# Rows along w without padding; the transform along h as 48-column products in two column halves

## The chip, the cores and the metric

One core of a Trainium2 chip runs the whole kernel. The metric is device time in microseconds (us); less is better. Data is float32 throughout, and a float32 product appears in the trace as two MATMUL records with a LDWEIGHTS record each, so a count of x14 stands for seven products. In this text such a record is called a pass.

## The reference

The input `x` is (2, 64, 64, 384): two images of 64 x 64 positions with 384 channels. Four spectral layers follow each other. Layers 0, 2 and 3 are alike; layer 1 uses a Hartley transform over all axes.

```python
xf = jnp.fft.rfft2(x, axes=(1, 2)).reshape(B, H, W // 2 + 1, 8, 48)      # 8 blocks of 48 channels
o1r = relu(einsum(xr, w1[0]) - einsum(xi, w1[1]) + b1[0])                # per block, 48 x 48
o1i = relu(einsum(xi, w1[0]) + einsum(xr, w1[1]) + b1[1])
o2r = einsum(o1r, w2[0]) - einsum(o1i, w2[1]) + b2[0]
o2i = einsum(o1i, w2[0]) + einsum(o1r, w2[1]) + b2[1]
out = irfft2(softshrink(o2r) + 1j * softshrink(o2i)) + x                 # layer 1: _dht instead
```

## The kernel before, in words

The kernel stays in the spectrum between layers. Phase A (about 0 to 360 us) transforms the input and does layer 0; phase B (to about 600 us) is layer 1; phase C is layers 2 and 3 and the inverse transform. The change touches only phase A.

The input is worked through in `PASSES = 4` passes: two images, and of each two halves of the channels (`PASS_C = 192` channels, that is two pairs of blocks). In a pass:

- **S1** (`s1`, L866, eight units `v` per pass) is the transform along w, as 64 x 64 products. Its result is copied from PSUM to a `stage` tile by `s1_views`: one half by ScalarE (L1159), one by VectorE (L1278). SyncE stores the stage to the DRAM tensor `rows_along_w` (`store_stage`, L586); of pass 0 GpSimd's queue stores half (L805).
- In `stage` and `rows_along_w` a channel pair takes `ROWS = 112` columns: 48 channels, 16 columns of padding, 48 channels. Two pairs make `PASS_ROWS = 224`. GpSimd zeroes the padding of the first four stage tiles once (L794, semaphore `pads_zeroed`), and the first S1 copies wait for that (L1127).
- `load_bm` (L594) reads six or seven columns of the w axis back into a `Bm` tile (three slots), now with h along the partitions.
- **S2** (`s2`, L889, 40 steps) is the transform along h. In it the data are the weights: for each of the `nk` columns (7 or 6) one product with `Bm(e)[:, at, cols]`, 128 x 112, as weights and a 128 x 128 constant `dft_h` as the moving operand. The result, 112 partitions x `nk` * 128, is copied by ScalarE to `modes_a(s)` (L1159).
- **S3** (`mix_first`, L901) and **S4** (`mix_second`, L910) are the two block products of layer 0. S3 reads partitions 0 to 47 and 64 to 111. **TA** (`turn`, L920) transposes the updated modes, **5A** (`s5`, L940) is the inverse along h, **6A** (`s6a`, L951) the inverse along w for layer 1.

The order is written out by hand in `order()`. A round r of phase A issues on TensorE: S2(r), TA(r-4), in some rounds S1 or 6A, S3(r-1), 5A, S4(r-2), in some rounds again S1 or 6A; then the next round. There are four PSUM units of two banks; each unit of work takes the next, once the work four places earlier has been copied out (`take`). Every engine runs its own part of this order, and semaphores tie them. PE passes of a unit follow each other with no wait in between.

On SyncE's queue, after the stores of pass 0: the constants, `load_bm(0)`, weights of layer 0, `load_bm(1)`, `load_bm(2)`, more constants, the four parts of the input of pass 1, weights for layer 1, `fwd_c`; then in round 2 `load_bm(3)`, which waits for S2(1) alone.

Of the kernel before, what the change touches and what calls it, by code (L numbers as in the profile page):

```python
# [4 lines left out]
BS = C // NB  # L5
P = 128
NT = C // P
HP = H // 2
# [7 lines left out]
HALF = 64  # L16
ROWS = HALF + BS
PAIRS = NB // 2
LAMBDA = 0.01

GROUPS = [7, 7, 7, 6, 6]
PASS_GROUPS = len(GROUPS)
PASSES = 2 * B
PASS_C = C // 2
PASS_PAIRS = PAIRS // 2
PASS_STEPS = PASS_GROUPS * PASS_PAIRS
PASS_ROWS = PASS_PAIRS * ROWS
STEPS = 2 * PASS_STEPS
ALL_STEPS = B * STEPS
ALL_GROUPS = PASSES * PASS_GROUPS  # L30
STEP_COLS = 2 * H * max(GROUPS)
ITEMS = 2 * PASS_GROUPS

X_PARTS = 4
X_HP = HP // X_PARTS
# [6 lines left out]
Y_SLOTS = 3  # L42
STAGE_SLOTS, BM_SLOTS, D_SLOTS, TURN_SLOTS, AN_SLOTS = 3, 3, 2, 2, 2
A_SLOTS = 7
C_SLOTS, R_SLOTS = 9, 4
# [207 lines left out]
    return parts, fwd_c.reshape(FOLD_ROWS + 1, -1).astype(np.float32), inv_c.reshape(P, -1).astype(np.float32)  # L253


STAGE_COLS = X_HP * PASS_ROWS
W3, W4 = 2 * PAIRS * ROWS, NB * 2 * HALF
FWD, INV, V3, V4 = 2 * 2 * 2 * P, 2 * 2 * (FOLD + 1), 2 * PAIRS * ROWS, NB * HALF

# [1 line left out]
def build(nc, x, consts, fwd_c_dram, inv_c_dram, conv_w3, conv_w4, conv_bias, l1_w3, l1_bias, l1_q, l1_e, l1_t,  # L261
# [11 lines left out]
    with ctx:  # L273
        def sb(name, n):
            return ctx.enter_context(nc.sbuf_tensor(name, [P, n], F32))

        def sem(name):
            return ctx.enter_context(nc.semaphore(name))

        def dram(name, shape):  # L280
            return nc.dram_tensor(name, shape, F32, kind="Internal").ap()
# [1 line left out]
        spectrum = dram("spectrum", (B, C + 1, KW, 2, H))  # L283
        flipped = dram("flipped", (B, C, MODES))
        update = dram("update", (B, 2, FOLD + 1, MODES))
        rows_along_w = dram("rows_along_w", (PASSES, P, HP, PASS_ROWS))
        rows_along_h = dram("rows_along_h", (2 * PASSES, 4, HP, HP, PASS_C))
        first_mix = dram("first_mix", (P, V3))
        second_mix = dram("second_mix", (ROWS, V4))

        X_AT, STAGE_AT = 0, X_PARTS * X_HP * PASS_C
        BM_AT, BM_COLS = STAGE_AT + STAGE_SLOTS * STAGE_COLS, max(GROUPS) * PASS_ROWS
        TURN_COLS = max(GROUPS) * PASS_C
        G_COLS = HP * PASS_C
        RX = sb("RX", BM_AT + BM_SLOTS * BM_COLS)
        RA = sb("RA", (A_SLOTS + 4) * STEP_COLS)
        RD = sb("RD", (D_SLOTS + TURN_SLOTS) * TURN_COLS)
        RG = sb("RG", 2 * G_COLS)
# [7 lines left out]
        def cst(name):  # L306
# [3 lines left out]
        identity, dft_w, dft_h, inv_w, inv_w_flip = (  # L310
            cst(n) for n in ("identity", "dft_w", "dft_h", "inv_w", "inv_w_flip"))
# [8 lines left out]
        def stage(p, k):  # L320
            if (p, k) == (0, X_PARTS - 1):
                return RD[:, D_SLOTS * TURN_COLS:D_SLOTS * TURN_COLS + STAGE_COLS]
            at = STAGE_AT + (p * X_PARTS + k) % STAGE_SLOTS * STAGE_COLS
            return RX[:, at:at + STAGE_COLS]

        def Bm(e):
            at = BM_AT + e % BM_SLOTS * BM_COLS
            lo, hi = columns_of(e)
            return RX[:, at:at + (hi - lo) * PASS_ROWS].rearrange("p (k r) -> p k r", r=PASS_ROWS)

        def D(e):
            at = e % D_SLOTS * TURN_COLS
# [32 lines left out]
            return RX[:, at:at + 2 * H * step_of(s)[3]]  # L365

        b_at = (C_SLOTS + R_SLOTS) * STEP_COLS
        assert BM_AT <= b_at

        OUT_COLS = X_HP * PASS_C  # L370

# [12 lines left out]
        N = STEP_COLS // 2  # L384
# [22 lines left out]
        an1_high, = in_region(RA, 3 * PAIRS * N, [PASS_PAIRS * N])  # L407
        assert Y_SLOTS * 4 * STEP_COLS + PASS_PAIRS * N <= b_at and 3 * PAIRS * N + PASS_PAIRS * N <= A_SLOTS * STEP_COLS
        an0, kf0, c0, c1 = in_region(RX, b_at, [PAIRS * N, PAIRS * N, N, N])
        assert Y_SLOTS * 4 * STEP_COLS <= BM_AT and b_at + 2 * PAIRS * N + 2 * N <= BM_AT + BM_SLOTS * BM_COLS  # L410
        kf1, r0, r1 = in_region(RD, 0, [PAIRS * N] * 3)
        assert 3 * PAIRS * N <= (D_SLOTS + TURN_SLOTS) * TURN_COLS
        raw0, s0, s1 = in_region(RA, 0, [PAIRS * N] * 3)
# [22 lines left out]
        prep, prep_at, at = {}, {}, 0  # L436
# [10 lines left out]
        psum = ctx.enter_context(nc.psum_tensor("psum", [P, UNITS * UNIT], F32))  # L447
# [5 lines left out]
        def banks(key):  # L453
            return unit(key).rearrange("p (a n) -> p a n", a=2)
# [5 lines left out]
        consts_loaded = sem("consts_loaded")  # L460
        inverse_loaded = sem("inverse_loaded")
        lambda_set = sem("lambda_set")
        pads_zeroed = sem("pads_zeroed")
        x_loaded = [sem(f"x_loaded{k}") for k in range(X_PARTS)]
        stage_stored = [sem(f"stage_stored{s}") for s in range(STAGE_SLOTS)]
        first_stage_stored = [sem(f"first_stage_stored{k}") for k in range(X_PARTS)]
# [97 lines left out]
        def stage_views(p, k, x):  # L564
            at = (4 * k + x) * X_HP
            return (rows_along_w[p, at:at + X_HP].rearrange("y q r -> q y r"),
                    stage(p, k)[x * HP:(x + 1) * HP].rearrange("q (y r) -> q y r", r=PASS_ROWS))

        block = ctx.enter_context(nc.Block())

# [214 lines left out]
        def _(pool):  # L785
# [3 lines left out]
                pool.dma_start(flipped[p // 2, c0:c0 + PASS_C // 2], AN(p, g)  # L789
                               ).then_inc(flipped_stored[(p * PASS_PAIRS + g) % AN_SLOTS], 16)  # L790

            for k in range(X_PARTS):
                pad = stage(0, k).rearrange("p (m r) -> p m r", r=ROWS)[:, :, BS:HALF]
                nc.gpsimd.memset(pad, 0.0).then_inc(pads_zeroed, 1)  # L794
            zeros = RN[0:KW, 0:2 * H]
            nc.gpsimd.memset(zeros, 0.0).then_inc(zero_set, 1)
            pool.wait_ge(zero_set, 1)
# [2 lines left out]
            for k in range(X_PARTS):  # L800
                wait_emptied(pool, ("S1", 0, 2 * k))
                wait_emptied(pool, ("S1", 0, 2 * k + 1))
                for x in range(2, 4):
                    dst, src = stage_views(0, k, x)
# [23 lines left out]
            for z in range(ITEMS):  # L828
                q, b = z // 2, z % 2
                n0, n = sum(GROUPS[:q]) * H, GROUPS[q] * H  # L830
                for t in range(2):
                    wait_emptied(pool, ("CI", z, t))
                for sign in range(2):
                    dst = update[b, sign, 0:FOLD, n0:n0 + n].rearrange("(t p) n -> p t n", t=2)
# [14 lines left out]
        def _(pe):  # L849
# [28 lines left out]
            def s2(s):  # L878
                key, e = ("S2", s), s // PASS_PAIRS
                _, g, k0, nk = step_of(s)  # L880
                bank = take(key)
                if s == 0:
                    pe.wait_ge(consts_loaded, 16)
                if s % PASS_PAIRS == 0:
                    wait_bm_loaded(pe, e)
                cols = slice(g % PASS_PAIRS * ROWS, (g % PASS_PAIRS + 1) * ROWS)
                for k in range(nk):
                    at, of = (max(k - 1, 0), k + 1 if k < 2 else 0) if k0 == 0 else (k, 0)
                    mm = nc.tensor.matmul(bank[0:ROWS, k * P:(k + 1) * P], Bm(e)[:, at, cols], dft_h[:, of * P:(of + 1) * P],  # L889
                                          start=True, stop=True)  # L890
                mm.then_inc(filled, 1)

            def mix_first(key, layer, n, src):
# [126 lines left out]
                mm.then_inc(filled, 1)  # L1020

            pe.wait_ge(dft_w_loaded, 16)
            for key in plan.order:
                stage = key[0]
                if stage == "S1":
# [58 lines left out]

        def s1_views(key, j):
            _, p, v = key
            n = 2 * PASS_ROWS
            at = j * (STAGE_COLS // 2) + v % 2 * n
            dst = stage(p, v // 2)[:, at:at + n].rearrange("p (m r) -> p m r", r=ROWS)
            dst = bass.AP(dst.tensor, dst.offset, [list(dst.ap[0]), [ROWS, n // ROWS], [HALF, 2], [1, BS]])  # L1090
            return dst, banks(key)[:, j, 0:2 * PASS_C].rearrange("p (m b c) -> p m b c", b=2, c=BS)

        def turn_views(key, first):
            _, s = key
# [29 lines left out]

        def wait_stage_free(eng, key):
            _, p, v = key
            if p == 0 and v == 0:  # L1127
                eng.wait_ge(pads_zeroed, X_PARTS)
            m = p * X_PARTS + v // 2 - STAGE_SLOTS
            if v % 2 == 0 and p > 0:  # L1130
                wait_stage_stored(eng, m // X_PARTS, m % X_PARTS)
# [144 lines left out]
        def _(vec):  # L1276
# [146 lines left out]
            def join_s(q):  # L1423
                vec.wait_ge(s_folded, 2 * B * (q + 1))
                n = GROUPS[q] * H
                for d, op in enumerate((ALU.add, ALU.subtract)):
                    for f in range(2):
                        nc.vector.tensor_tensor(s_sum[d][:, f, :, 0:n], s_of[0][:, f, :, 0:n], s_of[1][:, f, :, 0:n], op
                                                ).then_inc(s_joined, 1)

            nc.vector.memset(small[:, 0:1], -LAMBDA).then_inc(lambda_set, 1)
            nc.vector.memset(small[:, 1:2], -LAMBDA / 64).then_inc(lambda_set, 1)
            for key in plan.order:
                stage = key[0]
# [27 lines left out]
                elif stage == "TA":  # L1462
                    _, s = key
                    e = s // PASS_PAIRS
# [14 lines left out]
                elif stage in ("5A", "5C"):  # L1479
                    at = 0 if stage == "5A" else ALL_GROUPS  # L1480
# [13 lines left out]
                elif stage == "CF":  # L1494
                    _, z, h = key
                    n = GROUPS[z // 2] * H
# [10 lines left out]
                elif stage == "H2":  # L1507
                    _, z, h = key
                    q, b = z // 2, z % 2
                    n = GROUPS[q] * H  # L1510
                    r = shrunk(h, GROUPS[q]).rearrange("p (a n) -> p a n", a=2)
# [165 lines left out]
```

## Time and profile before

| | before |
|---|---|
| median of 3 runs | 1030.41 us (1029.93 to 1033.44) |
| the profiled execution | 1035.22 us, of it the span of the trace 1033.4 us |
| TensorE busy (matmul) | 925.4 us, 90% |
| TensorE busy (weight load, beside matmul) | 466.4 us, 45% |
| VectorE, ScalarE, GpSimd busy | 574.3, 476.5, 80.7 us |
| chain that ended last, by engine | PE 79%, DMA 10%, DVE 4%, issue 3% |
| L889 (S2) matmul | x528, 71.0 us busy, 21.1 us idle just before |
| DMA moved | 184.39 MB in 94255 packets |

The profiled execution took 4.8 us more than the median. Engines are PE (TensorE matmul), PEld (its weight load), DVE (VectorE), ACT (ScalarE), POOL (GpSimd), SP (SyncE). The profile gives for groups of instructions their busy time, the mean duration of one, and the idle time of their engine just before them with what ended it.

### The profile page before, as it was taken

Reading aid. Unit: us, or ns where it says so; the run is one execution under the profiler, and the core shown is the slowest. Engines: PE = TensorE matmul, PEld = TensorE weight load, DVE = VectorE, ACT = ScalarE, POOL = GpSimd, SP = SyncE. Lnnn points to the kernel's source line nnn. Section 1 sums busy time; section 2 is a strip of 40 time slices with the busy share of each in tenths; the row PEclk is TensorE's granted clock in tenths of the full one; section 3 lists DMA queues with packets and bytes.
Section 4 is the critical chain, followed back from the end, with each engine's and each line's share of the span. In section 5 each row is a group of like instructions: output and inputs, shape, how many; then the busy total and the mean of one; then the engine's idle time right before and its main releaser. Section 6 shows DMA issues by size and latency. Waiting matters only on the chain.

```text
span 1033.4 us, 14264 instructions
## 1 busy us (share of the span) xinstructions
PE 925.4 (90%) x5168; PEld 466.4 (45%) x5168; DVE 574.3 (56%) x869; ACT 476.5 (46%) x757; POOL 80.7 (8%) x157
## 2 busy tenths in 40 slices
PE   3879999999999989499999999999999999999812
PEld 1536556665766646144444434443433434344301
DVE  1245554454544847476775676665667656656411
ACT  1435445545544424133343445655565655556501
POOL 3011111111111100000000110000000000000001
PEclk8889999999999999799999999999999999999966
DMA  8976699478658696934333443442754566451464
GB/s 277 328 204 187 249 286 356 136 201 293 224 159 281 197 313 166 210 90 123 96 105 89 128 128 106 103 131 77 237 138 138 159 211 177 137 204 49 130 127 184
DMA packets 94255, 184.39 MB, mean 178 GB/s; under 512 B 12455, under 2 KB 72129, under 8 KB 92394
## 3 DMA queue, kind: packets, MB, share of 16 engines
q1 hardware_dynamic: 84362, 142.33, 47.1%
q0 software_dynamic: 9824, 41.14, 12.1%
q8 instruction: 43, 0.70, 0.3%
q14 instruction: 26, 0.21, 0.1%
HBM read 104.29 MB, written 79.14 MB: 177 GB/s over the span
## 4 chain that ended last, share of the span: by engine, by line
PE 79%; DMA 10%; DVE 4%; issue 3%; ACT 2%; SPq 1%; DVEq 0%; POOL 0%; ACTq 0%; POOLq 0%
PE psum L910 16%; PE psum L901 16%; PE psum L940 9%; PE psum L889 6%; PE psum L977 6%; PE psum L993 6%; PE psum L1017 6%; PE psum L920 5%; PE psum L951 4%; DMA RX<-rows_along_w 4%; PE psum L1004 3%; DMA RG<-rows_along_h 3%; PE psum L866 2%; DMA RX<-spectrum 1%; ACT RA L1174 1%
## 5 line engine op out<-in xcount | busy, mean ns | idle before, releaser
L1318 DVE SCALAR_TENSOR_TENSOR RA<-psum,RA 112x896 f32<-112x896 f32 (+1 forms) x120 | 124.3, 1036 | 221.6 <-ACT RA L1174 221.4
L1174 ACT ACTIVATE RA<-psum,small 112x896 f32<-112x896 f32 (+1 forms) x120 | 115.9, 966 | 96.8 <-PE psum L910 94.3
L910 PE MATMUL psum<-RA,RW 112*64 112x448 f32 (+1 forms) x640 | 132.4, 535 | 1.4 <-ACT RA L1165 1.4
L1165 ACT ACTIVATE RA<-psum,RW 112x448 f32<-112x448 f32 (+1 forms) x160 | 89.4, 610 | 79.3 <-PE psum L901 79.3
L940 PE MATMUL psum<-RD,const 128*128 128x384 f32 (+1 forms) x304 | 100.0, 450 | 9.9 <-DVE RA L1278 5.3
L1278 DVE COPY RD<-psum 128x672 f32<-128x672 f32 (+2 forms) x122 | 69.7, 572 | 67.0 <-PE psum L940 60.7
L1159 ACT ACTIVATE RA<-psum 128x384 f32<-128x384 f32 (+2 forms) x72 | 50.6, 704 | 86.5 <-PE psum L889 59.1
L889 PE MATMUL psum<-const,RX 128*112 128x128 f32 x528 | 71.0, 289 | 21.1 <-DMA RX<-rows_along_w 21.1
L1159 ACT ACTIVATE RD<-psum 128x384 f32<-128x384 f32 (+2 forms) x122 | 64.1, 526 | 39.6 <-PE psum L940 37.8
L1303 DVE TENSOR_TENSOR RX<-RX,RA 112x768 f32<-112x768 f32 (+2 forms) x80 | 80.7, 1009 | 1.5
L889 PEld LDWEIGHTS psum<-const,RX 128*112 128x112 f32 x528 | 63.6, 186 | 39.7 <-issue 33.2
L940 PEld LDWEIGHTS psum<-RD,const 128*128 128x128 f32 x304 | 51.2, 192 | 63.7 <-issue 29.2
L910 PEld LDWEIGHTS psum<-RA,RW 112*64 112x64 f32 x640 | 39.1, 136 | 77.0 <-issue 68.6
L901 PE MATMUL psum<-RX,RN 48*112 48x448 f32 (+1 forms) x320 | 66.9, 535 | 5.8 <-issue 4.3
L901 PE MATMUL psum<-RA,RW 48*112 48x448 f32 (+1 forms) x320 | 67.0, 537 | 2.7 <-ACT RX L1159 1.7
L1165 ACT ACTIVATE RA<-psum,RN 112x448 f32<-112x448 f32 (+1 forms) x80 | 44.7, 610 | 49.1 <-PE psum L901 49.1
L901 PE MATMUL psum<-RX,RW 48*112 48x448 f32 (+1 forms) x320 | 67.0, 537 | 0.0
L910 PE MATMUL psum<-RA,RN 112*64 112x448 f32 (+1 forms) x320 | 65.2, 528 | 0.9 <-ACT RA L1165 0.9
L816 POOL DMA_DIRECT2D spectrum<-RA x80 | 40.1, 505 | 302.2 <-DVE RA L1303 213.4
L1224 ACT ACTIVATE RA<-psum,small 112x448 f32<-112x448 f32 (+1 forms) x80 | 44.7, 610 | 38.4 <-PE psum L993 38.4
L1159 ACT ACTIVATE RN<-psum 96x264 f32<-96x264 f32 (+4 forms) x52 | 30.6, 588 | 67.7 <-PE psum L1017 42.0
L977 PE MATMUL psum<-RG,RF 96*128 96x448 f32 (+3 forms) x160 | 61.8, 530 | 0.0
(102 smaller groups left out, 1092.7 us busy)
## 6 DMA issues: line engine op xcount, KB each, us to landing
RG<-rows_along_h SPq DMA_DIRECT2D x7, 3072.0 KB, 11.7
rows_along_h<-RD SPq DMA_DIRECT2D x96, 144.0 KB, 2.9
RX<-x SPq DMA_DIRECT2D x16, 768.0 KB, 8.0
out<-RA POOLq DMA_DIRECT2D x16, 768.0 KB, 4.5
rows_along_w<-RX SPq DMA_DIRECT2D x54, 224.0 KB, 5.3
rows_along_h<-RD SPq DMA_DIRECT2D x64, 168.0 KB, 3.1
RX<-rows_along_w SPq DMA_DIRECT2D x12, 672.0 KB, 6.8
spectrum<-RA POOLq DMA_DIRECT2D x48, 168.0 KB, 5.1
```

Source lines behind the costliest of these rows:

```text
L889: mm = nc.tensor.matmul(bank[0:ROWS, k * P:(k + 1) * P], Bm(e)[:, at, cols], dft_h[:, of * P:(of + 1) * P], start=True, stop=True)
L901: mm = nc.tensor.matmul(dst, w3[layer][rows, a, g], src[rows, :, a], start=a == 0, stop=a == 1)
L910: mm = nc.tensor.matmul(bank[b * HALF:(b + 1) * HALF, a * BANK:a * BANK + nk * H], w4[layer][0:ROWS, g, b, a], hidden(slot)[0:ROWS, b * N: ...
L940: mm = nc.tensor.matmul(dst, matrix[:, 0:P], d[:, at:at + hi - lo], start=True, stop=True)
L977: mm = nc.tensor.matmul(bank[:, part * BANK:part * BANK + n], fwd_c_view[rows, t, part, m], uv[d][rows, part, t, 0:n], start=t == 0, stop= ...
L993: mm = nc.tensor.matmul(bank[0:ROWS, r * BANK:r * BANK + n], v3_view[rows, s, g], src[rows, 0:n], start=s == 0, stop=s == 1)
L1159: return nc.scalar.activation(dst, src, ACT.Copy)
L1165: done = nc.scalar.activation(hidden(slot)[0:ROWS, b * N:b * N + nk * H], banks(key)[0:ROWS, b, 0:nk * H], ACT.Relu, bias=bias[layer][0:RO ...
L1174: nc.scalar.activation(dst, src, ACT.Relu, bias=minus_lambda_l0 if key[0] == "S4" else minus_lambda).then_inc(act_emptied, 1)
L1278: return nc.vector.tensor_copy(dst, src)
L1303: last = nc.vector.tensor_tensor(m[:, :, k], m[:, :, k], src[:, :, k], ALU.add)
L1318: nc.vector.scalar_tensor_tensor(out=dst, in0=src, scalar=LAMBDA / 64 if key[0] == "S4" else LAMBDA, in1=dst, op0=ALU.add, op1=ALU.min).th ...
```

## The change

A channel pair is carried in 96 columns, without the 16 of padding. Stage, `rows_along_w` and `Bm` shrink from 224 to 192 columns per row. In S2 each product of 112 weight columns becomes two of 48, one per channel block: block 0 writes PSUM partitions 0 to 47, block 1 partitions 64 to 111, of the same bank and columns, with the same moving operand. The partitions between (48 to 63) are no longer written by S2, so VectorE clears partitions 32 to 63 of all of PSUM once at the start (semaphore `psum_cleared`, for which TensorE waits before its first product); GpSimd's four memsets and `pads_zeroed` go. S1's copies write a contiguous destination. The tile `RX` keeps its size by another expression.

```diff
-PASS_ROWS = PASS_PAIRS * ROWS
-STAGE_COLS = X_HP * PASS_ROWS
+STAGE_COLS = X_HP * PASS_C
-        rows_along_w = dram("rows_along_w", (PASSES, P, HP, PASS_ROWS))
+        rows_along_w = dram("rows_along_w", (PASSES, P, HP, PASS_C))
-        BM_AT, BM_COLS = STAGE_AT + STAGE_SLOTS * STAGE_COLS, max(GROUPS) * PASS_ROWS
+        BM_AT, BM_COLS = STAGE_AT + STAGE_SLOTS * STAGE_COLS, max(GROUPS) * PASS_C
...
-            for k in range(X_PARTS):
-                pad = stage(0, k).rearrange("p (m r) -> p m r", r=ROWS)[:, :, BS:HALF]
-                nc.gpsimd.memset(pad, 0.0).then_inc(pads_zeroed, 1)
...
-                cols = slice(g % PASS_PAIRS * ROWS, (g % PASS_PAIRS + 1) * ROWS)
                 for k in range(nk):
                     at, of = (max(k - 1, 0), k + 1 if k < 2 else 0) if k0 == 0 else (k, 0)
-                    mm = nc.tensor.matmul(bank[0:ROWS, k * P:(k + 1) * P], Bm(e)[:, at, cols], dft_h[:, of * P:(of + 1) * P],
-                                          start=True, stop=True)
+                    for b in range(2):
+                        c0 = (g % PASS_PAIRS * 2 + b) * BS
+                        mm = nc.tensor.matmul(bank[b * HALF:b * HALF + BS, k * P:(k + 1) * P], Bm(e)[:, at, c0:c0 + BS],
+                                              dft_h[:, of * P:(of + 1) * P], start=True, stop=True)
...
+            pe.wait_ge(psum_cleared, 1)
...
-            n = 2 * PASS_ROWS
+            n = 2 * PASS_C
             at = j * (STAGE_COLS // 2) + v % 2 * n
-            dst = stage(p, v // 2)[:, at:at + n].rearrange("p (m r) -> p m r", r=ROWS)
-            dst = bass.AP(dst.tensor, dst.offset, [list(dst.ap[0]), [ROWS, n // ROWS], [HALF, 2], [1, BS]])
-            return dst, banks(key)[:, j, 0:2 * PASS_C].rearrange("p (m b c) -> p m b c", b=2, c=BS)
+            return stage(p, v // 2)[:, at:at + n], banks(key)[:, j, 0:n]
...
-            if p == 0 and v == 0:
-                eng.wait_ge(pads_zeroed, X_PARTS)
...
+            nc.vector.memset(psum[32:HALF, :], 0.0).then_inc(psum_cleared, 1)
             nc.vector.memset(small[:, 0:1], -LAMBDA).then_inc(lambda_set, 1)
```

## Rows read from the trace of the kernel before

**Rows 1.** Busy time by stretch: PE, PEld, DVE, ACT, POOL; granted clock, DMA share, GB/s.
```profile
10.00:25.30 15.30, 3.77 (x40) 1.51 (x32) 3.20 (x6) 2.80 (x6) 6.02 (x10) 0.76 0.96 272
...
100.00:360.00 260.00, 257.80 (x1783) 161.33 (x1780) 137.47 (x217) 127.48 (x197) 35.25 (x70) 1.00 0.74 239
```

**Rows 2.** PE's waits from 70.5 to 360 us: total, times, longest.
```profile
PE psum L889 <- DMA RX<-rows_along_w: 5.1, 1, 5.1
PE psum L951 <- DVE RN L1278: 0.9, 2, 0.7
```

**Rows 3.** The chain that ended last, pieces of its first 75 us: start, us, what.
```profile
5.67 8.14 PE psum L866 x64
...
18.59 6.54 DMA rows_along_w<-RD
25.27 4.37 DMA RX<-rows_along_w
29.78 5.87 PE psum L889 x28
35.68 34.68 DMA RX<-rows_along_w
70.50 2.87 PE psum L889 x12
```

**Rows 4.** DMA issues: queue, count, KB each, median us from issue to landing.
```profile
rows_along_w<-RX SPq DMA_DIRECT2D x54, 224.0 KB, 5.3
...
RX<-rows_along_w SPq DMA_DIRECT2D x12, 672.0 KB, 6.8
...
RX<-rows_along_w SPq DMA_DIRECT2D x8, 784.0 KB, 9.3
```

**Rows 5.** PE groups by shape (weights, then moving operand): count, busy us, mean ns, idle before.
```profile
L910 PE MATMUL psum<-RA,RW 112*64 112x448 f32 x384 | 84.1, 559 | 1.4 <-ACT RA L1165 1.4
...
L966 PE MATMUL psum<-RG,const 64*64 64x384 f32 x256 | 28.2, 538 | 22.3 <-DMA RG<-rows_along_h 22.3
```

**Rows 6.** PE and PEld around one S4 unit and the S2 after it: start, us, passes.
```profile
40.67 0.20 PEld L910 LDWEIGHTS psum<-RA,RW 112*64 112x64 f32 x4 [0.67 <-ACT RA L1159]
40.67 0.60 PE L910 MATMUL psum<-RA,RW 112*64 112x448 f32 x2
40.67 1.72 PE L910 MATMUL psum<-RA,RW 112*64 112x448 f32 x8
41.10 0.14 PEld L910 LDWEIGHTS psum<-RA,RW 112*64 112x64 f32 x2 [0.23 <-issue]
42.33 1.78 PE L889 MATMUL psum<-const,RX 128*112 128x128 f32 x14
```

**Rows 7.** PE, two stretches: of phase A, 286 to 295 us, and of phase C, 717 to 722 us.
```profile
286.34 1.56 PE L940 MATMUL psum<-RD,const 128*128 128x384 f32 x4
...
289.49 1.57 PE L951 MATMUL psum<-const,RG 128*96 128x66 f32 x16
290.90 1.73 PE L889 MATMUL psum<-const,RX 128*112 128x128 f32 x14
292.46 0.74 PE L920 MATMUL psum<-const,RA 112*128 112x112 f32 x6
...
717.70 1.72 PE L910 MATMUL psum<-RA,RW 112*64 112x448 f32 x8
719.25 1.67 PE L910 MATMUL psum<-RA,RN 112*64 112x448 f32 x8
720.86 0.89 PE L920 MATMUL psum<-const,RX 112*128 112x112 f32 x7
```

**Rows 8.** VectorE's first instruction, and two of its PSUM copies by shape (count, busy, mean ns).
```profile
0.81 0.06 DVE L1431 MEMSET small<- 128x1 f32 x1 [0.81 <-PEq L1667]
...
L1278 DVE COPY RD<-psum 128x672 f32<-128x672 f32 x2 | 1.7, 844 | 0.0
L1278 DVE COPY RD<-psum 128x384 f32<-128x384 f32 x2 | 1.1, 558 | 0.2
```

More of the change, by code:

```diff
@@ L291, in build @@
         X_AT, STAGE_AT = 0, X_PARTS * X_HP * PASS_C
-        BM_AT, BM_COLS = STAGE_AT + STAGE_SLOTS * STAGE_COLS, max(GROUPS) * PASS_ROWS
+        BM_AT, BM_COLS = STAGE_AT + STAGE_SLOTS * STAGE_COLS, max(GROUPS) * PASS_C
         TURN_COLS = max(GROUPS) * PASS_C
         G_COLS = HP * PASS_C
-        RX = sb("RX", BM_AT + BM_SLOTS * BM_COLS)
+        RX = sb("RX", max(BM_AT + BM_SLOTS * BM_COLS, (C_SLOTS + R_SLOTS + 5) * STEP_COLS))
         RA = sb("RA", (A_SLOTS + 4) * STEP_COLS)
@@ L328, in Bm @@
             lo, hi = columns_of(e)
-            return RX[:, at:at + (hi - lo) * PASS_ROWS].rearrange("p (k r) -> p k r", r=PASS_ROWS)
+            return RX[:, at:at + (hi - lo) * PASS_C].rearrange("p (k r) -> p k r", r=PASS_C)
         def D(e):
@@ L367, in build @@
         b_at = (C_SLOTS + R_SLOTS) * STEP_COLS
-        assert BM_AT <= b_at
         OUT_COLS = X_HP * PASS_C
@@ L409, in build @@
         an0, kf0, c0, c1 = in_region(RX, b_at, [PAIRS * N, PAIRS * N, N, N])
-        assert Y_SLOTS * 4 * STEP_COLS <= BM_AT and b_at + 2 * PAIRS * N + 2 * N <= BM_AT + BM_SLOTS * BM_COLS
+        assert Y_SLOTS * 4 * STEP_COLS <= BM_AT and b_at + 2 * PAIRS * N + 2 * N <= (C_SLOTS + R_SLOTS + 5) * STEP_COLS
         kf1, r0, r1 = in_region(RD, 0, [PAIRS * N] * 3)
@@ L462, in build @@
         lambda_set = sem("lambda_set")
-        pads_zeroed = sem("pads_zeroed")
+        psum_cleared = sem("psum_cleared")
         x_loaded = [sem(f"x_loaded{k}") for k in range(X_PARTS)]
@@ L566, in stage_views @@
             return (rows_along_w[p, at:at + X_HP].rearrange("y q r -> q y r"),
-                    stage(p, k)[x * HP:(x + 1) * HP].rearrange("q (y r) -> q y r", r=PASS_ROWS))
+                    stage(p, k)[x * HP:(x + 1) * HP].rearrange("q (y r) -> q y r", r=PASS_C))
         block = ctx.enter_context(nc.Block())
```

## Prediction

> **What bounds the kernel now.** I read three views first. The busy times by stretch say where TensorE has slack: from 100 to 360 us it is busy 257.8 of 260 us at full clock, while the DMA engines are at 0.74 [rows 1]. Then PE's own waits in phase A: behind 70 us they come to under 7 us, of which one of 5.1 us is for a `Bm` load, and the next in size is 0.9 us in two places [rows 2]. Then the chain that ended last, followed through the first 75 us [rows 3]: after S1 it is DMA up to 29.78 us (stores of the stage, landed at 25.1, then the first `Bm` load), TensorE to 35.68, and once more a `Bm` load, issued at 35.68 and used at 70.50. So phase A has two limits. Until 70.5 us the transfers decide: from 10 to 25.3 us the DMA engines are busy 0.96 of the time at 272 GB/s [rows 1]. After that the sum of TensorE's units decides, and every 0.1 us added to or taken from a unit goes straight to the end, 40 rounds long.
>
> The change acts on both: fewer bytes early, and other work for TensorE in each of the 40 S2 units.
>
> **Part 1, the products of S2.** What is S2 bound by? A unit of 14 passes takes 1.78 us, of which about 0.27 is the tail of the last pass, so a pass comes every (1.78 - 0.27) / 14 = 0.108 us [rows 6]. The 5A unit of full width: 4 passes of 384 moving columns in 1.56 us, (1.56 - 0.28) / 4 = 0.32 us per pass, or 0.83 ns per column [rows 7]; 128 columns times that is 0.107. So S2 is bound by the 128 moving columns, not by its 112 weight columns. Two products of 48 weight columns stream the same 128 columns twice. If they ran one after the other, S2's time would double; if the two column halves of the array work side by side, it stays.
>
> The nearest row is S4 (L910): 64 weight columns, outputs at partitions 0 and 64 of the same bank, the two halves next to each other in program order. Eight passes of 448 columns take 1.72 us; at 0.83 ns per column one pass needs 0.373 us, so eight in a row would take 3 us. The window of 0.1 us from the start of the unit already holds two passes, and a weight load of two more runs at 41.10 beside the matmuls [rows 6]. Over the whole run it is 84.1 / 384 = 0.219 us per pass; with four quarters (the inverse along w of phase C, L966, 64 x 64) it is 28.2 / 256 = 0.110 us per pass of 384 columns, against the 0.32 of full width [rows 5, 7]. The array runs tiles at different output partitions at once. S2's new products differ from S4's in three points: 128 instead of 112 contraction rows, 48 instead of 64 columns, and a stream of 128 instead of 448, so that 4 passes and 4 loads must be fed per 0.215 us. Feeding is no problem by the same rows: 4 loads and the 2 first passes begin within 0.1 us. I take the pair's pitch at 0.108 us as before, and +0.3 us in 40 units for the second half starting a few ns later. Bounds of this part: 0 and, if serial, 264 products x 2 passes x 0.108 = +57 us.
>
> **Part 2, the neighbours of S2.** Going from one shape of tile to another costs TensorE a pause. S4 before S2: its streams end at 40.67 + 0.05 (first load) + 4 x 0.375 (a pair of passes: 448 columns at 0.83 ns and 2 ns) = 42.22, S2 begins at 42.33, 0.10 later, and then takes 1.78 us, where the S2 behind a 6A of full width takes 1.73 [rows 6, 7]. S2 before TA, both of full width: TA begins at 292.46, 1.56 after S2's start, just when 14 x 0.109 and a part of the first load are over: no pause [rows 7]. Two units in column halves: 717.70 + 0.05 + 1.50 = 719.25, the next begins at 719.25, and takes 1.67 instead of 1.72. A turn behind column halves: 719.25 + 1.50 = 720.75, it begins at 720.86, 0.10 later, and takes 0.89 us for 7 passes, where 0.74 for 6 and one more of 0.10 make 0.84 [rows 7]. After the change S2 belongs to the column halves. By the order:
> - S2 to TA, 36 times, 34 of them behind 70 us: + (0.10 + 0.05) x 34 = +5.1 us.
> - S4 to S2, 17 times, 16 behind 70 us: the pause of 0.10 goes, and so does the exposed first load of 112 columns, 0.09 (1.78 less 0.27 less 13 x 0.109): -0.19 x 16 = -3.0 us.
> - 6A to S2, 9 times: a pause of 0.10 instead of some 0.03, and 0.04 of first load as before: +0.07 x 9 = +0.6 us.
> - S1 (or the one weight product) to S2, 8 times behind 70 us: the pause stays, the exposed load shrinks from 0.09 to 0.04: -0.4 us.
>
> With the 0.3 of part 1 that is +2.6 us. These sit on the path, since PE doesn't wait there [rows 2]; what falls before 70 us is swallowed by the wait for the load. Bounds: 0, if all is absorbed, and +6 us, if nothing is saved at S4 to S2.
>
> That such a pause exists is also what the Trainium skill states, in TensorEngine Tiling (Array Packing), section Key Properties: a change of tiling mode drains the engine, a change of tile within one mode does not. It gives no figure, and the rows here agree with both halves of it; the sum goes by the rows.
>
> **Part 3, the bytes.** Each row goes from 224 to 192 columns, one seventh less. Sixteen stores of pass 0 at 224 KB [rows 4] are 3.67 MB, 0.52 MB less after; at 272 GB/s [rows 1] that is 1.9 us of the stretch that ends at 25.1 us. Of the first `Bm` load, 672 KB in 4.37 us from issue to use [rows 3, 4], 0.1 MB goes: 0.2 us. If time went by number of pieces and not by bytes it would be 0, as the count stays. Bounds 0 to 2.3; I take 2.1, since that stretch is at the DMA engines' limit. The second place is the load issued at 35.68. It stands behind everything queued since 25 us, so it shifts with the start (the 2.1 again, not added), and 0.33 MB less lies in front of it and in it: at 272 GB/s up to 1.2 us, at the least 0; I take 0.7. TensorE itself arrives there 2.1 us earlier, so the wait stays, some 4.5 us long instead of 5.1, and what is won by both is 2.8 us. Behind it nothing in phase A waits on a transfer, so the lighter DMA traffic there is worth 0.
>
> **Part 4, the start.** VectorE clears 4096 columns on 32 partitions before anything else. Its copies of 672 and 384 columns out of PSUM take 844 and 558 ns [rows 8]: 0.99 ns per column, so 4096 take about 4.2 us, from 0.81 to 5.0. TensorE's first pass waits for the input until 5.67 [rows 3]; this covers it with 0.5 us to spare. ScalarE's `lambda_set` comes 4.2 us later and is not needed before the first S1 result at 7.4. If the clearing took twice as long, the start would move by 3.7 us, though part of it would go into stores that wait for the DMA engines anyway. The memsets that GpSimd loses had ended before 2 us and nobody waited on them. S1's copies keep their 384 elements: 0. The copy of S2 keeps its shape: 0.
>
> **Sum,** on the profiled execution of 1035.22 us: -2.8 + 2.6 = -0.2 us. Moved to the median of the runs shown, 4.8 us lower: 1030.4 - 0.2 = 1030.2 us. About 0.5% (5 us) is what a measurement can tell from no change here.
>
> **Rivals.**
> 1. Serial halves (slower). If two products of 128 rows over the same moving columns don't share the array, S2 doubles: +57 us, 1087. For it: no row shows 128 contraction rows in column halves, or one operand streamed into both. Against it: S4 does it with 112 rows. It decides from the first S2 on.
> 2. Weight loads no longer hidden. With a stream of only 0.107 us and a load of 48 columns on each side, a load that can't overlap adds its 0.04 us (6A: 16 passes of 96 weight columns in 1.57 us, 0.083 each and longer than the 0.055 of its 66 moving columns, so 0.86 ns per weight column [rows 7]): 528 x 0.04 = +21 us, 1051. Against it: the load at 41.10 runs beside matmuls in S4. This is what a rule of the Trainium skill would give (TensorE: Matmul & The Clock Gate, the mechanism of packing small matmuls: weight loads overlap matmuls in flight only where the row groups differ). In S4 all row groups are shared and the load overlaps, so the trace speaks against it.
> 3. The early transfers give more. If the load at 35.68 lands early enough that the 5.1 us wait goes, and S2 behind it runs at 2.4 instead of 1.2 GHz (2.87 us for 12 passes against 1.73 for 14), it is 5.1 + 1.3 + 2.1 - 2.6 = -6 us, 1024. Against it: 0.33 MB can't pay for 5 us.
> 4. The change saves bytes but not time (time by pieces): 0 + 2.6, 1033. This lies within the forecast's case.
>
> **How the numbers follow.** Forecast with rival 4, that is all within 0.5%: 0.74. Rival 3: 0.10. Rival 1: 0.08; rival 2: 0.04; the clearing at the start or more pauses than counted, beyond +5 us: 0.04. So faster by over 0.5% 0.10, same 0.74, slower 0.16. The parts' own bounds reach from -3.5 to +6 us; rival 3 extends the lower end. The range is 1023.5 to 1036.5 us.
>
> **What would show it.** L889 at x1056 with a busy time near 71 us and two passes beginning together; an S2 of seven columns in about 1.7 us. Near 130 us busy would be rival 1, near 92 rival 2. TA behind S2 at 0.79 us and 0.1 us later; S4 to S2 with no pause. First S2 at about 27.7 us, the seventh at about 67.7. A first S1 pass later than 5.7 us would mean that the clearing isn't covered.

## The result and the profile after

The change makes the kernel slower by 0.2 to 0.3%: 1034.62 us (median of 20 runs) against 1031.86 (20 runs), a ratio of 1.0031 [1.0017, 1.0044]. The same kernel timed twice more, each time beside the kernel before, gave 1.0012 [0.9998, 1.0026] and 1.0018 [1.0007, 1.0030]; weighted by their intervals the three make 1.0020 ± 0.0007, or +2.1 ± 0.8 us. Executions in a slow state with a lower granted clock (one of `e10_flips_together` with 1561.73 us, one of the kernel before with 1052.01) are left out of all ratios. The forecast was -0.2 us. The time is inside the range of 1023.5 to 1036.5 us and inside the half per cent called "same", but the effect is clear of zero, and it has the other sign.

The profiled execution of after took 1034.76 us (span 1033.0), that of before 1035.22. The two profiles therefore don't show the difference; the profiled before lay 3.4 us above the median of its kernel, the profiled after on it. What they do show is each step by itself. First the page of after: busy times, DMA totals, and S2 (L885 now, L889 before) with its weight loads.

```profile
PE 924.8 (90%) x5696; PEld 464.0 (45%) x5696; DVE 577.8 (56%) x870; ACT 476.4 (46%) x757; POOL 79.5 (8%) x153
...
DMA packets 94131, 180.26 MB, mean 175 GB/s; under 512 B 12455, under 2 KB 72001, under 8 KB 92266
...
L885 PE MATMUL psum<-const,RX 128*48 128x128 f32 x1056 | 68.9, 284 | 20.6 <-DMA RX<-rows_along_w 20.6
L885 PEld LDWEIGHTS psum<-const,RX 128*48 128x48 f32 x1056 | 61.0, 128 | 36.0 <-issue 29.1
```

Twice as many passes, 1056, hold TensorE for 68.9 us. That is 0.065 us a pass, where 128 columns take 0.107 us to stream: the two halves work side by side. Next, TensorE around an S2 behind an S4, and around one behind a 6A and ahead of TA (start, us, line, weights, moving operand, passes).

```profile
38.52 1.72 PE L906 MATMUL psum<-RA,RW 112*64 112x448 f32 x8
40.08 1.70 PE L885 MATMUL psum<-const,RX 128*48 128x128 f32 x28
...
288.91 1.57 PE L947 MATMUL psum<-const,RG 128*96 128x66 f32 x16
290.42 1.74 PE L885 MATMUL psum<-const,RX 128*48 128x128 f32 x28
292.08 0.79 PE L916 MATMUL psum<-const,RA 112*128 112x112 f32 x6
```

S4 to S2 is 1.56 us from start to start, 1.66 before, and S2 takes 1.70 instead of 1.78 [rows 6]. 6A to S2 is 1.51, 1.41 before; S2 to TA is 1.66, 1.56 before; TA takes 0.79 instead of 0.74 [rows 7]. Then VectorE's first instructions, the chain that ended last up to the seventh S2, and PE's waits from 68.7 to 360 us.

```profile
1.66 3.47 DVE L1424 MEMSET psum<- 32x4096 f32 x1 [1.66 <-PEq L1661]
5.13 0.06 DVE L1425 MEMSET small<- 128x1 f32 x1
```

```profile
5.58 7.21 PE psum L861 x64
...
16.73 6.91 DMA rows_along_w<-RD
...
23.77 3.90 DMA RX<-rows_along_w
...
27.80 5.74 PE psum L885 x56
...
33.58 34.92 DMA RX<-rows_along_w
...
68.63 2.80 PE psum L885 x24
```

```profile
PE psum L885 <- DMA RX<-rows_along_w: 5.6, 1, 5.6
PE psum L897 <- issue: 1.0, 2, 0.6
PE psum L947 <- DVE RN L1271: 0.9, 2, 0.7
```

The clearing ends at 5.13 us and the first pass comes at 5.58, no later than before (5.67). The first S2 starts at 27.80 instead of 29.78 us and the seventh at 68.63 instead of 70.50 [rows 3]; the wait for the second load stays. By these views Parts 1, 2 and 4 went as forecast, and of the 2.8 us of Part 3 the seventh S2 has 1.9. The last 5A unit but one starts at 366.31 us in after and at 366.30 in before: at the end of phase A this pair of profiles has the change at nothing, as forecast. The question is why the timed kernel still loses 2 us.

### The profile page after: what moved, and what is told of

Read it like the earlier page. It is cut to its first block, busy times and chain, and to the rows that moved or that the text cites. A ratio compares the mean times of both kernels' runs of the same rounds, so it can differ in the third digit from the quotient of the medians.

```text
span 1033.0 us, 15316 instructions
## 1 busy us (share of the span) xinstructions
PE 924.8 (90%) x5696; PEld 464.0 (45%) x5696; DVE 577.8 (56%) x870; ACT 476.4 (46%) x757; POOL 79.5 (8%) x153
## 4 chain that ended last, share of the span: by engine, by line
PE 80%; DMA 9%; DVE 4%; issue 3%; ACT 2%; SPq 1%; POOL 0%; ACTq 0%; DVEq 0%; POOLq 0%
PE psum L897 16%; PE psum L906 16%; PE psum L936 8%; PE psum L973 6%; PE psum L989 6%; PE psum L1013 6%; PE psum L885 6%; PE psum L916 5%; PE psum L947 4%; DMA RX<-rows_along_w 4%; PE psum L1000 3%; DMA RG<-rows_along_h 3%; PE psum L861 2%; PE psum L962 2%; DMA RX<-spectrum 1%
## 5 line engine op out<-in xcount | busy, mean ns | idle before, releaser
L936 PE MATMUL psum<-RD,const 128*128 128x384 f32 (+1 forms) x304 | 97.6, 442 | 9.9 <-DVE RA L1271 5.3
L885 PE MATMUL psum<-const,RX 128*48 128x128 f32 x1056 | 68.9, 284 | 20.6 <-DMA RX<-rows_along_w 20.6
L885 PEld LDWEIGHTS psum<-const,RX 128*48 128x48 f32 x1056 | 61.0, 128 | 36.0 <-issue 29.1
```

The costliest lines, as they stand in the source:

```text
L885: mm = nc.tensor.matmul(bank[b * HALF:b * HALF + BS, k * P:(k + 1) * P], Bm(e)[:, at, c0:c0 + BS], dft_h[:, of * P:(of + 1) * P], start=Tr ...
L936: mm = nc.tensor.matmul(dst, matrix[:, 0:P], d[:, at:at + hi - lo], start=True, stop=True)
```

## The experiments

All ratios are to the kernel before, timed beside each kernel. Code cuts leave out lines that say nothing new; `...` stands for what is skipped inside a line or between lines.

**The parts one by one.** `e1_split_padded` is the kernel before with S2 split and the padding kept:

```
+ pe.wait_ge(psum_cleared, 1)
+ nc.vector.memset(psum[32:HALF, :], 0.0).then_inc(psum_cleared, 1)
...
- mm = nc.tensor.matmul(bank[0:ROWS, ...], Bm(e)[:, at, cols], ...)
+ for b in range(2):
+     c0 = g % PASS_PAIRS * ROWS + b * HALF
+     mm = nc.tensor.matmul(bank[b * HALF:b * HALF + BS, ...], Bm(e)[:, at, c0:c0 + BS], ...)
```

> The kernel before with only S2 cut into two products of 48 columns in the two column halves (and the clearing at the start); rows keep their padding, so transfers are those of before. Theory A (the pauses between shapes of tile cost, the bytes gain, both as the traces show them): first S2 at 29.8 us as before, then a drift of +2 us up to 360 us, and 2 us more in the time, ratio 1.002. Theory B (the bytes' gain of 2 us does not reach the end): the ratio is that of the whole change, 1.003, since the bytes count for nothing. Theory C (the cause is where the tensors lie in DRAM and on chip after the rows shrank): the drift of 2 us again but no more than that, while the whole change costs 3 or more on top of its gain.

Measured: 1036.30 us, 1.0034 [1.0019, 1.0049]. The split by itself, clearing included, costs 3.5 ± 1.5 us. The 1.002 of theory A and the 1.003 of theory B both lie in its interval.

`e2_narrow_whole` is the change without the split, one product over 96 unpadded columns; the clearing stays, on partitions 96 to 127 in place of 32 to 63:

```
- for b in range(2):
-     c0 = (g % PASS_PAIRS * 2 + b) * BS
-     mm = nc.tensor.matmul(bank[b * HALF:b * HALF + BS, ...], Bm(e)[:, at, c0:c0 + BS], ...)
+ c0 = g % PASS_PAIRS * 2 * BS
+ mm = nc.tensor.matmul(bank[0:2 * BS, ...], Bm(e)[:, at, c0:c0 + 2 * BS], ...)
```

> The changed kernel with one product of 96 weight columns to partitions 0 to 95 in S2 in place of the two of 48: the bytes alone, no column halves. The second block of each pair lands on partitions 48 to 95 where the later steps don't look for it, so layer 0 and what follows are computed on other channels. Theory A: first S2 at 27.8 us and no drift, 2 us less than before, ratio 0.998. Theory B: 1.000, the gain is lost behind 360 us. Theory C: 1.001 to 1.003, slower although TensorE's part is back.

Measured: 1031.04 us, 0.9989 [0.9977, 1.0000].

`e3_placement` gives the changed kernel the memory layout of before: a spare DRAM tensor of the missing size and `RX = sb("RX", 16224)`. `e4_after_again` is the changed kernel.

> The changed kernel with everything back at its old place: a spare DRAM tensor of the size that rows_along_w lost, and RX at its old 16224 columns. Theories A and B: as the changed kernel, ratio to before 1.003. Theory C: 1.000 or below, the 3 us go.

> The changed kernel as it is, on the same chip and beside the same runs of before. All theories: 1.003, between 1.0017 and 1.0044; its second trace shows which waits differ from execution to execution. If it comes out within 0.001 of 1, the difference depends on the chip, and nothing else in this set can be read to 2 us.

Measured: 1033.37 us, 1.0008 [0.9995, 1.0020], and 1034.45 us, 1.0012 [0.9998, 1.0026]. e3 lies between the 1.000 of theory C and the 1.003 of theories A and B, but so does e4, the same kernel with its buffers where the change puts them: where they lie makes no difference that these runs can tell. (Taken as a fourth timing of the changed kernel, e3 brings the mean to 1.0017 ± 0.0006, or +1.8 ± 0.7 us.)

`e5_before_again` is the kernel before; `e6_clear_only` adds to it the clearing and TensorE's wait for it (the first two lines of e1); `e7_bytes_whole_112` takes the rows without padding and keeps one product of 112 columns, without clearing:

```
+ c0 = g % PASS_PAIRS * (PASS_C - ROWS)
+ mm = nc.tensor.matmul(bank[0:ROWS, ...], Bm(e)[:, at, c0:c0 + ROWS], ...)
```

> The kernel before, unchanged, taken as if it were an experiment: ratio 1.000 within 0.001, and a second trace of it. Theory A (the traces tell the whole difference; the one trace of before at hand was itself of a slow execution, by some 2.5 us in phases B and C): from the first unit of phase C to the last 5C about 377 us instead of 379.2, a span near 1031. Theory B (something behind 360 us is slower in the changed kernels): the second trace repeats 379.2 and a span near 1033.

> The kernel before with only the clearing of partitions 32 to 63 of PSUM at the start and TensorE's wait for it. If the clearing is covered by the input's way in, as the trace of the changed kernel shows (it ends at 5.13 us, the first product at 5.58): ratio 1.000. Rival: the clearing ends after the input in many executions, or VectorE's late start delays what follows: up to +1 us, ratio 1.001, and part of the 3.4 us of the split kernel is explained by it.

> The changed kernel with S2 as one whole product of 112 weight columns as before, read from the unpadded rows (columns 0 to 111 for the first pair, 80 to 191 for the second, so the second block of a pair and others are not where layer 0 expects them: other channels are computed), and without the clearing: the bytes alone and nothing else of the change. Theory A: first S2 at 27.8 us, the seventh at 68.4, no drift against before, ratio 0.998 (2.4 us less). Theory B: 0.999 to 1.000, the gain of the start is lost later.

Measured: 1033.57 us, 1.0005 [0.9986, 1.0024]; 1033.07 us, 1.0006 [0.9993, 1.0020]; 1031.46 us, 0.9988 [0.9973, 1.0003]. The clearing can't be told from nothing. e2 and e7 agree; together the smaller rows are worth 0.9989 ± 0.0009, which is -1.2 ± 0.9 us, where -2.8 was forecast. The second trace of before has a span of 1033.0 us, not the 1031 of theory A; but e6, which adds only the clearing, has 1029.2, so one span decides nothing.

The profiled executions of the whole kernel can't settle a microsecond. Here are TensorE's granted clocks (second last but two of the columns) in two stretches, first of before and then of e6, whose work is the same there:

```profile
360.00:370.00 10.00, 7.30 (x32) 4.76 (x31) 8.98 (x12) 1.95 (x4) 2.03 (x4) 0.83 0.98 303
...
700.00:712.00 12.00, 10.45 (x48) 4.16 (x44) 6.38 (x13) 5.84 (x9) 0.00 (x0) 0.86 0.36 99
```

```profile
360.00:370.00 10.00, 7.30 (x35) 4.72 (x34) 8.70 (x12) 1.95 (x4) 2.03 (x4) 1.00 1.01 322
...
700.00:712.00 12.00, 10.45 (x52) 4.68 (x53) 8.56 (x16) 6.45 (x12) 0.00 (x0) 1.00 0.44 126
```

In the one execution the clock fell to the lower of its two levels (1.2 GHz) for a part of both stretches, in the other it stayed at 2.4 GHz. From the start of the last 5A unit but one, near 366 us, to that of a late 5C unit, near 979, executions took between 609.7 and 614.1 us, kernels with and without the change mixed. At that 5A unit four traces of the changed kernel (after, e3, e4, e12) stand at 366.2 us in the mean and three of before (before, e5, e6) at 366.5; their spans are 1032.0 and 1031.9 us. So no trace shows where the 2 us of the timed runs arise, and with spans that scatter by 4 us none excludes them.

**Phase A alone.** The next kernels end behind phase A and write sixteen stores of one x part as output. `e13_cut_before` is cut out of before, `e14_cut_after` out of after, `e15_cut_split_padded` out of e1, `e16_cut_bytes` out of e7. The cut in `order()` and at the end (the edit also takes out what only phases B and C need, and waits for the last stores):

```
  if 0 <= r - ALL_STEPS - 4 < 2:
-     o += [("CF", 0, r - ALL_STEPS - 4)]
+ return o
...
+ for p in range(PASSES):
+     for k in range(X_PARTS):
+         pool.dma_start(out[p, k], X(0)).then_inc(out_stored[0], 16)
```

> The kernel before, cut off behind the last 5A of phase A: layer 1 to 3 and the inverse transform are left out, and as output 16 copies of one input part are stored once the last modes are written (the same work in all four kernels of this set). It is the base of the set; its time, some 400 us, should scatter less than a whole run, since the waits of phases B and C are gone.

> The changed kernel, cut off in the same way. If the loss of 2 us is made in phase A, only not visible in the traces: 2 us more than the cut kernel before. If phase A is what the traces say (five traces with unpadded rows, three with padded and whole S2): 0.3 us less, within 1 us of it, and the loss comes from phases B and C, which the change does not touch.

> The kernel of e1 (S2 in column halves, rows padded), cut off in the same way. By the traces 1.6 us more than the cut kernel before; by the timed whole runs 3.4 us more.

> The kernel of e7 (unpadded rows, S2 whole, other channels computed), cut off in the same way. By the traces 1.6 to 2.4 us less than the cut kernel before; by the timed whole runs 1.2 us less.

Measured: 417.80, 419.91, 420.08 and 417.83 us, each to about ±1 us by its interval. At face value the split costs 2.3 us and the change as a whole 2.1, and the smaller rows bring 0.0, each to about ± 1.2 us. But the trace of e16 shows the gain: its seventh S2 starts at 68.47 us against 70.69 in e13, its last 5A unit but two at 359.06 us against 360.92. The end of the chain in e13 and e16, and the landing of the output stores:

```profile
364.09 8.39 POOL out L760 x16
out<-RX POOLq DMA_DIRECT2D x16, 768.0 KB, 21.9
```

```profile
362.22 8.43 POOL out L755 x16
out<-RX POOLq DMA_DIRECT2D x16, 768.0 KB, 23.5
```

The stores are issued 1.9 us earlier in e16, and the median one lands 1.6 us later after its issue. From 376 to 388 us the DMA engines are busy 1.02 of the time in both: the tail that I had put there is limited by transfers, and it is the likely place where the gain went. The same tail stands behind e14 and e15, so their 2.1 and 2.3 us are no clean measure either: the stores of e14 are issued only 0.8 us later than those of e13 (364.92 against 364.09), while its span is 2.3 us longer (417.9 against 415.6). No kernel with the short tail was made of the change or of the split. So `e17_short_before` and `e18_short_bytes` are e13 and e16 with one store:

```
- for p in range(PASSES):
-     for k in range(X_PARTS):
-         pool.dma_start(out[p, k], X(0)).then_inc(out_stored[0], 16)
+ pool.dma_start(out[0, 0], X(0)).then_inc(out_stored[0], 16)
```

> The kernel before, cut behind phase A like e13_cut_before, and with one store of one x part at the end in place of sixteen (everything behind phase A is left out, and of the output only one part is written). It is the base for e18_short_bytes: about 366 to 370 us by either theory, since the sixteen stores took what e13 ran beyond its last product of phase A.

> e16_cut_bytes (rows without padding, S2 as one product, no clearing) with one store at the end in place of sixteen. Theory M, the smaller loads do bring the products of phase A forward by what the traces show, 1.9 to 2.4 us, and in e16 the stores behind it swallowed that: 1.9 to 2.4 us under e17_short_before. Rival N, the gain is a matter of the profiled executions and isn't there in timed runs, as e16 against e13 (0.0 us) suggests: within 0.5 us of e17_short_before.

Measured: 385.24 us, ratio 0.3725 [0.3716, 0.3734], and 382.85 us, 0.3707 [0.3699, 0.3715]: the ratios differ by 0.0018 ± 0.0012, or 1.9 ± 1.2 us. (Both took some 15 us more than expected: in the trace of e17 the stores of `rows_along_h` are issued until 376.5 us, behind the last products, and still have to land.) The second load in the chain of e17 and of e18:

```profile
25.93 4.13 DMA RX<-rows_along_w
...
34.93 35.98 DMA RX<-rows_along_w
```

```profile
23.92 3.92 DMA RX<-rows_along_w
...
33.27 34.90 DMA RX<-rows_along_w
```

It is issued 1.66 us earlier, lands another 1.08 us sooner, and both reach TensorE: the seventh S2 starts at 68.30 us against 71.05. So timed runs have the gain of the smaller rows too, if nothing at the end covers it. These two traces also show waits for a transfer behind the seventh S2, in e17 and then in e18, which before doesn't have:

```profile
PE psum L864 <- DMA RG<-rows_along_h: 1.8, 2, 0.9
```

```profile
PE psum L859 <- DMA RG<-rows_along_h: 1.0, 1, 1.0
```

**Does the number of products cost anything?** `e11_quarters` makes four products of 32, 16, 32 and 16 weight columns out of the two; `e12_after_third` is the changed kernel beside it.

```
- for b in range(2):
-     c0 = (g % PASS_PAIRS * 2 + b) * BS
+ for to, c, n in ((0, 0, 32), (32, 32, 16), (64, 48, 32), (96, 80, 16)):
+     c0 = g % PASS_PAIRS * 2 * BS + c
```

> The changed kernel with S2 in four products of 32, 16, 32 and 16 columns at partitions 0, 32, 64 and 96: the same result, twice the instructions of S2 once more (2112 passes). By the pauses alone: the four run side by side, the pass stays at 0.109 us, and S4 to S2 becomes a change of shape again: 17 x 0.14 = 2.4 us more than the changed kernel, ratio to before 1.0045. Rival D (each further instruction costs by itself, and that is why the split costs 3.4 us in the timed runs and 1.6 in the traces): 2 us more on top, or a pass above 0.115 us, ratio 1.0065 or more. Rival E (quarters don't run side by side): S2 doubles, +57 us, 1.055.

> The changed kernel a third time, beside the same runs of before as the others. If the loss is real and about 2 us, as the mean of the ratios 1.0031 and 1.0012 says: 1.001 to 1.003. If the traces' sum holds (bytes -2.4, S2 and its neighbours +1.6 to +2): 0.999 to 1.000.

Measured: 1035.85 us, 1.0039 [1.0023, 1.0054], and 1034.36 us, 1.0018 [1.0007, 1.0030]. The same S4 and S2 in e11 and in e12:

```profile
113.76 1.51 PE L906 MATMUL psum<-RA,RW 112*64 112x384 f32 x8
115.20 1.73 PE L885 MATMUL psum<-const,RX 128*32 128x128 f32 x56
116.86 0.79 PE L916 MATMUL psum<-const,RA 112*128 112x112 f32 x6
```

```profile
113.07 1.51 PE L906 MATMUL psum<-RA,RW 112*64 112x384 f32 x8
114.41 1.70 PE L885 MATMUL psum<-const,RX 128*48 128x128 f32 x28
116.04 0.79 PE L916 MATMUL psum<-const,RA 112*128 112x112 f32 x6
```

56 passes take 1.73 us where 28 take 1.70: passes as such are nearly free. But S4 to S2 is 1.44 us again instead of 1.34. The neighbours no longer share a shape, halves of 64 columns against quarters of 32, and the pause of 0.10 us is back, 16 times. With 0.03 us more in each of 33 S2 units that is 2.6 us; from the eighth S2 to the fortieth it is 258.9 us in e11 against 256.4 in e12. Timed, e11 is 2.2 ± 2.0 us above e12. Rival E (quarters one after the other) is out, and rival D (each instruction costs by itself) as well, with a pass every 31 ns and a ratio of 1.0054 at most.

**The order of the shapes.** If pauses between shapes are what the split costs, an order with fewer of them wins. `e8_turn_behind_mix` is the changed kernel with TA and the first 6A unit of a round moved behind S3. TA then stands next to 6A and 5A, which are of full width like itself, and a round has three changes of shape instead of four (S2 to S3, S3 to TA, 5A to S4). In `order()`:

```
  if r < ALL_STEPS:
      o += [("S2", r)]
- if 0 <= r - 4 < ALL_STEPS:
-     o += [("TA", r - 4)]
...
+ if 0 <= r - 1 < ALL_STEPS:
+     o += [("S3", r - 1)]
+ if 0 <= r - 4 < ALL_STEPS:
+     o += [("TA", r - 4)]
  for p in range(PASSES - 1):
      if 0 <= r - flip_round(p) < FLIP_UNITS:
          o += [("6A", p, 0, r - flip_round(p))]
- if 0 <= r - 1 < ALL_STEPS:
-     o += [("S3", r - 1)]
```

> The changed kernel with the turn TA (and the 6A behind it) moved behind S3 in every round, so that TA, 6A and 5A, all of full width, follow each other: one change of tile shape less per round. If each change costs its 0.15 us on the path (0.10 of pause and 0.05 of exposed first load): 36 rounds x 0.15 = 5.4 us less than the changed kernel, about 1029 us, ratio to before near 0.997. Rival: ScalarE now empties S2 and S3 back to back, its work becomes the bound of the round and the gain is below 2 us.

Measured: 1025.51 us, 0.9933 [0.9915, 0.9951], faster than both kernels. `e9_order_only` has this order with before's S2 and padding, and `e10_flips_together` has, on top of e8, both 6A units of a round next to each other.

> The kernel before with only the order of e8 (S3 ahead of TA and 6A), S2 whole and rows padded. If the gain of e8 is the changes of tile shape: here S2 has full width and S3 behind it half the rows, so the number of changes per round stays that of before, and only the waits for ScalarE in rounds with S1 (0.6 to 1.1 us, four places, 2.8 us in all) can go: ratio about 0.997, drift of phase A down by 2 to 3 us. If it is the order as such, whatever the shapes: 0.993 as e8.

> e8 with the second 6A of a round put right behind the first, in place of behind S4. Twelve rounds lose two changes of shape (S4 to 6A and 6A to S2, 0.10 to 0.19 us each): 12 x 0.3 = 3 us less than e8, ratio to before 0.990. Rival: two 6A units in a row wait for their copies out (four copies of 0.3 to 0.6 us by two engines against 1.3 us of TensorE each), gain 0 to 1 us.

Measured: 1030.47 us, 0.9983 [0.9973, 0.9993], and 1026.04 us, 0.9940 [0.9927, 0.9953]. e10 brings nothing beyond e8 where 3 us were expected. Its trace has the last 5A unit but one 1.5 us earlier than e8's, 357.72 against 359.20 us, and only 0.4 us of that in the span; I didn't follow it further. A stretch of after and one of e8 without 6A units between S2 and S4 (the first line of e8 has only the last 16 of the 28 passes of its S2, which begins at 294.13 us):

```profile
299.84 1.74 PE L885 MATMUL psum<-const,RX 128*48 128x128 f32 x28
301.50 0.89 PE L916 MATMUL psum<-const,RA 112*128 112x112 f32 x7
302.32 1.76 PE L897 MATMUL psum<-RA,RW 48*112 48x448 f32 x8
304.01 1.56 PE L936 MATMUL psum<-RD,const 128*128 128x384 f32 x4
305.50 1.72 PE L906 MATMUL psum<-RA,RW 112*64 112x448 f32 x8
```

```profile
294.82 1.04 PE L885 MATMUL psum<-const,RX 128*48 128x128 f32 x16
295.79 1.76 PE L897 MATMUL psum<-RA,RW 48*112 48x448 f32 x8
297.48 0.89 PE L916 MATMUL psum<-const,RA 112*128 112x112 f32 x7
298.21 1.47 PE L936 MATMUL psum<-RD,const 128*128 128x384 f32 x4
299.61 1.72 PE L906 MATMUL psum<-RA,RW 112*64 112x448 f32 x8
```

In after TA to the next unit is 0.82 us, in e8 0.73; 5A to S4 is 1.49 in after and 1.40 in e8, since nothing stands between TA and 5A that has another shape. One change of shape less saves 0.09 + 0.09 = 0.18 us in a round, over 34 rounds 6.1 us. The measured difference of e8 to the changed kernel is 0.0087, 9 ± 2 us. The order has some gain beside the shapes: with S2 in one product it has four changes of shape in a round as before, and e9 still gained 1.8 ± 1.0 us. The traces agree: from the eighth S2 to the fortieth it is 249.5 us in e8 against 256.4 in after, and 251.9 in e9 against 254.6 in before. That is 6.8 and 2.7 us, and leaves some 4 us for the shapes, less than the 6.1 counted. What makes the 2 to 3 us of the order alone was not taken apart.

## Why the prediction was wrong

**Part 1, right.** The halves run side by side and the weight loads are hidden: 28 passes of 48 columns in 1.70 to 1.74 us where 14 passes of 112 took 1.73 to 1.78. Serial halves would have shown near 130 us busy for L885, unhidden loads near 92; it is 68.9 against the 71 written down. Rivals 1 and 2 are out. Rival 2 was also what the Trainium skill gives (TensorE: Matmul & The Clock Gate, on packing small matmuls: a weight load overlaps matmuls in flight only where the row groups differ). These two halves share all row groups, and the trace contradicts the rule for them: with an exposed 0.04 us in 28 passes S2 would take near 2.3 us instead of 1.7. The same section of the Trainium skill also lets a load ahead that goes to the background weight buffer; the traces here don't tell in which way the loads are hidden.

**Part 2, right row by row; its sum is less sharply measured.** S2 to TA was priced at +0.15 us: it is 0.10 from start to start and 0.05 in TA. S4 to S2 was priced at -0.19: -0.10 and -0.08. 6A to S2, priced at +0.07, is +0.10. S1 to S2, priced at -0.05, is -0.04 (the eighth S2 takes 1.52 us in place of 1.56). Parts 1 and 2 together were to cost 2.6 us; e1 measured 3.5 ± 1.5 with the clearing, and e15 2.3 ± 1.2 with the tail that spoils it. The traces have less: from the eighth S2 to the fortieth it is 254.6 us in before and 256.4 in after, 1.8 us more, and five traces of the changed kernel (e14 with them) agree on that 256.4 within 0.02. e11 confirms the mechanism in the other direction: take away the equal shape of S4 and S2 and the saved pause comes back. The Trainium skill's rule that a change of tiling mode drains the engine and a change of tile within a mode does not (TensorEngine Tiling (Array Packing), Key Properties) holds in all these rows; it gives no size, the rows give 0.10 us.

**Part 3 failed: the term of -2.8 us.** At its place it was nearly right. Five traces with padding and one product in S2 (before, e5, e6, e13, e17) have the first S2 at 29.8 us in the mean, four without padding (e2, e7, e16, e18) at 28.0, 1.8 earlier (forecast 2.1); the seventh is at 70.8 against 68.3, 2.5 earlier (forecast 2.8). What failed is the next step, that all of this arrives at the end of the kernel: the timed whole kernels have 1.2 ± 0.9 of it (e2 and e7), the timed short ones 1.9 ± 1.2 (e18 against e17). In the traces it does live to the end of phase A: the same nine have the fortieth S2 at 336.9 and 334.4 us, again 2.5, though single pairs of them lie between 1.4 and 3.2 us apart. So where the 1.6 us between 2.8 and 1.2 go is not settled: the intervals of 1.9 ± 1.2 and 1.2 ± 0.9 overlap, and a loss behind phase A has not been shown.

Two things behind the seventh S2 that the prediction put at nothing do move by about a microsecond from execution to execution. One is the transfers, behind which "nothing in phase A" was to wait: e17, e18 and e7 wait 1.8, 1.0 and 0.3 us for `RG`. The other is TensorE's clock after its wait for the second load. In before, after 5.1 us without work, it stays at 0.50 (1.2 GHz) until 76 us, in e13, the same work after 6.5 us without any, only until somewhere between 73 and 74. The TA behind the seventh S2 in before and in e13:

```profile
73.16 1.51 PE L920 MATMUL psum<-const,RA 112*128 112x112 f32 x7
```

```profile
73.35 1.04 PE L835 MATMUL psum<-const,RA 112*128 112x112 f32 x7
```

From the seventh S2 to the eighth it is 11.56 us in before and 10.40 in e13, 11.61 in e7 and 10.92 in e16. A gain of 2.5 us can lose or win half of itself there.

Three smaller slips. 0.1 MB less in the first load is 0.36 us at 272 GB/s, not the 0.2 that was taken (4.37 us became 3.90). In Part 4 a clearing twice as long would have moved the start by 3.5 us, not 3.7. And TensorE's waits behind 70.5 us add up to 7.3 us in before, not to under 7, with 0.7 us of ScalarE and 0.6 of "issue" beside the rows shown.

**Part 4, right.** The clearing took 3.47 us, 0.85 ns per column instead of the 0.99 taken from the PSUM copies, and began at 1.66 instead of 0.81 us. Both misses cancel: it ended at 5.13 (5.0 written), 0.45 us ahead of the first pass. e6 finds no cost, 0.6 ± 1.4 us.

**The sum.** With the terms as the timed kernels have them, -1.2 ± 0.9 and +3.5 ± 1.5, it is +2.3 ± 1.7 us, and 2.1 ± 0.8 was measured. Of the miss of 2.3 us Part 3 makes 1.6; the other 0.9, 3.5 in place of 2.6, lies within the interval of e1. My -0.2 was the difference of two terms of the same size and could have no sign of its own. It rested on taking from Part 3 a value near the upper bound of the gain, 2.8 of 3.5 us, while Part 2 was taken in its middle. Rival 4, no time for the bytes, gave +2.6 and lies nearest to the measurement, though its reason was wrong: the bytes do save time. Rival 3 did not occur; the wait for the second load stayed, at 5.6 us.

## What to carry to other kernels

Where TensorE has no slack, count the changes of tile shape in its order, not only its passes: each cost 0.10 us of pause and up to 0.09 of exposed first load here, and sorting the same work so that equal shapes stand next to each other took the ratio from 1.0020 to 0.9933 (some 2 of these 9 us come with the order even without the shapes, by e9). Time won early by a smaller transfer should be entered in the sum at the lower part of its bounds until something later has been seen to receive it. A kernel cut short for measurement needs a tail that is itself not limited by what is measured: behind sixteen output stores the smaller rows gained 0.0 ± 1.2 us, behind one 1.9 ± 1.2.

## What was not expected of the hardware

Four products of 32 and 16 weight columns work side by side as well as two of 48 (56 passes in 1.73 us), so neither the number of matmuls nor that of weight loads was a limit down to one pass per 31 ns (1.73 / 56). Halves next to quarters cost the same pause, 0.10 us, as halves next to full width. And two executions of one program may differ in TensorE's clock at the same work: from 700 to 712 us the granted clock was 0.86 in e4 and 1.00 in after, the same kernel; whole profiles lay up to 4.4 us apart behind phase A (609.7 to 614.1), too far to read a difference of 2 from them.
